# Three value blocks moved in the hand-written plan of an attention loop, and a layer norm's scale made of operations with one tensor

## What is computed

```python
xn = layernorm(x)                                  # x: 4 sequences x 1024 tokens x 1024
# s: causal attention on xn, 32 heads of 32, 8 key/value heads, rotary positions
scores = q @ k.T / sqrt(32); attn = softmax(causal(scores)); s = (attn @ v) @ wo.T
# g: a small recurrent network on the last token of each sequence (4 rows)
x_norm  = layer_norm(xn, in_gamma, in_beta)
thought = x_norm[:, -1, :] @ agg_w + agg_b
for _ in range(4):                                 # 4 steps
    t = layer_norm(thought, pn_gamma, pn_beta)     # its scale is what the change touches
    t = gelu(t @ d1_w + d1_b)                      # 1024 -> 4096
    thought = thought + (t @ d2_w + d2_b)          # 4096 -> 1024
broadcast = thought @ bc_w + bc_b
out = xn + sigmoid(xn @ gate_w + gate_b) * broadcast
g = silu(layer_norm(out, out_gamma, out_beta))
result = x + s * g
```

## Time and profile before

| | |
|---|---|
| time, median of 3 runs | 2708.13 us (2706.33 to 2709.1) |
| the profiled execution's own time | 2710.05 us |
| its span | 2708.0 us |
| PE busy | 2565.2 us, 95% |
| DVE busy | 1760.8 us, 65% |
| ACT busy | 1016.2 us, 38% |
| POOL busy | 1369.7 us, 51% |
| mean granted clock of PE | 0.978 |

### The profile page before, as it was taken

One profiled execution on the slowest core, in us unless ns is written; L12 is line 12 of the kernel. 1 busy time (PEld: TensorE's weight loads), 2 busy tenths in 40 slices (PEclk: granted clock), 3 DMA queues, 4 the chain that ended last, 5 costly groups with the idle time before them and its releaser, 6 DMA issues. The chain is left out here.

```text
span 2708.0 us, 45646 instructions
## 1 busy us (share of the span) xinstructions
PE 2565.2 (95%) x14400; PEld 1702.8 (63%) x14400; DVE 1760.8 (65%) x3577; ACT 1016.2 (38%) x1650; POOL 1369.7 (51%) x627
## 2 busy tenths in 40 slices
PE   5999999988999989999999999999859999999998
PEld 4888888863444444444444544444348888888886
DVE  6444444436676676677676676676756777777777
ACT  2111111102566656566566655665431111111111
POOL 1111111123888878988888987988711111111111
PEclk9999999997999989999999999999979999999999
DMA  6444444437456546556456555456375666655566
GB/s 239 173 179 178 173 165 163 164 119 250 154 163 189 176 134 195 160 162 188 131 178 198 166 157 182 149 167 194 114 221 117 123 128 126 119 116 116 116 116 124
DMA packets 228288, 432.05 MB, mean 160 GB/s; under 512 B 16472, under 2 KB 98520, under 8 KB 228176
## 3 DMA queue, kind: packets, MB, share of 16 engines
q1 hardware_dynamic: 154784, 378.74, 42.5%
q0 software_dynamic: 73392, 51.91, 12.6%
HBM read 316.56 MB, written 113.51 MB: 159 GB/s over the span
## 5 line engine op out<-in xcount | busy, mean ns | idle before, releaser
L883 DVE CUSTOM_DVE_ANT_0 bcast<-mxp,mask_q 128x128 f32<-128x128 f32 (+7 forms) x1054 | 753.3, 752 | 368.9 <-PE mxp L1001 192.6
L800 ACT ACTIVATE pr<-stp 128x512 f32<-128x512 f32 x1152 | 665.5, 597 | 542.8 <-PE stp L1008 343.2
L1008 PE MATMUL stp<-qs,ks 97*128 97x512 f32 x1152 | 515.1, 458 | 33.6 <-ACT pr L800 25.3
L427 PE MATMUL eo<-xt,w 128*128 128x512 f32 x1920 | 449.6, 394 | 3.6 <-DVE xt L370 3.6
L751 POOL TENSOR_TENSOR acc<-acc,pr 128x2048 f32<-128x2048 f32 x96 | 440.3, 4587 | 9.3 <-ACT pr L800 4.8
L1008 PEld LDWEIGHTS stp<-qs,ks 97*128 97x128 f32 x1152 | 216.0, 190 | 359.3 <-ACT pr L800 252.7
L427 PEld LDWEIGHTS eo<-xt,w 128*128 128x128 f32 x1920 | 359.6, 189 | 77.4 <-issue 4.0
L1371 PE MATMUL gp<-g,xa 128*128 128x512 f32 x1536 | 355.5, 391 | 17.6 <-DMA xa<-xt_scratch 17.6
L1371 PE MATMUL op<-o,ya 128*128 128x512 f32 x1536 | 355.4, 391 | 10.9 <-DVE ya L1314 10.9
L1371 PEld LDWEIGHTS gp<-g,xa 128*128 128x128 f32 x1536 | 289.8, 189 | 78.7 <-DMA xa<-xt_scratch 18.5
L1371 PEld LDWEIGHTS op<-o,ya 128*128 128x128 f32 x1536 | 289.7, 189 | 71.6 <-DVE ya L1314 11.4
(11 more groups left out here) (139 smaller groups left out, 2895.8 us busy)
## 6 DMA issues: line engine op xcount, KB each, us to landing
wch<-in_d_w SPq DMA_DIRECT2D x132, 1024.0 KB, 9.8
qs<-q_scratch SPq DMA_DIRECT2D x201, 256.0 KB, 7.3
xa<-xt_scratch POOLq DMA_DIRECT2D x66, 512.0 KB, 6.3
xt_scratch<-xt SPq DMA_DIRECT2D x16, 2048.0 KB, 14.0
q_scratch<-r SPq DMA_DIRECT2D x64, 512.0 KB, 3.2
yr<-y_scratch POOLq DMA_DIRECT2D x33, 512.0 KB, 5.8
xs<-in_x SPq DMA_DIRECT2D x33, 512.0 KB, 5.5
y_scratch<-ys SPq DMA_DIRECT2D x65, 256.0 KB, 2.0
```

Of the source, the lines that this page charges most:

```text
L427: last = nc.tensor.matmul(out, lhs[a](k), rhs[c](k), start=(k == 0 and (a, c) == (0, 0)), stop=(k == KT - 1 and (a, c) == (1, 0)))
L800: nc.scalar.activation(pr[half][:, :, at:at + P], stp[u % 2][:].rearrange("p (h t) -> p h t", h=REP), ACT.Exp, scale=SCALE).then_inc(act_d ...
L883: last = nc.vector.tensor_tensor_reduce(out=bcast[:, k % 2, hh * step:hh * step + w], in0=mxp[k % 2][:, hh * step:hh * step + w], in1=mask ...
L1008: last = nc.tensor.matmul(bank, ks[par][:, j * P:(j + 1) * P], qs[par][:, :, i * P:(i + 1) * P], start=True, stop=i != j)
```

## The change

Three value blocks stand in other slots of the plan: (1,0) goes from slot 18 to slot 22, (1,1) from 23 to 22, and (1,2) from 23 to 28. Their order doesn't change, and neither do the slots of anything else.

The layer norm's scale was three operations on 128x32 elements, each with two tensors (the second one spread out by a step of 0). It becomes four operations on 128x8 elements, one for each row r, that multiply with the one number `rs[:, r]` of each partition, and then eight on 128x4, one for each kk, that multiply with one number of each partition and add another. Only one wait of DVE for itself stands within them, where two did.

```diff
--- before.py
+++ after.py
@@ -82,17 +82,16 @@
 15: mx 6
 16: ss 1, rc 1
 17: mx 7
-18: pv 1 0
 19: mx 8, l0, lc, ge
 20: mx 9
 21: ss 0, rc 0
-22: mx 10
-23: mx 11, pv 1 1, pv 1 2
+22: mx 10, pv 1 0, pv 1 1
+23: mx 11
 24: mx 12, l1, lv
 25: mx 13
 26: mt 0
 27: mx 14
-28: mx 15, pv 1 3
+28: mx 15, pv 1 2, pv 1 3
 29: mx 16
 30: mx 17
 31: pv 1 4
@@ -858,9 +857,13 @@
 
             def layernorm_scale(k, base):
                 dve.wait_ge(ln_rs, k + 1)
-                link(nc.vector.tensor_tensor(cen[:], cen[:], rows(rs[:]), ALU.mult), base)
-                link(nc.vector.tensor_tensor(cen[:], cen[:], bc(fvec[:, 1, :], B), ALU.mult), base)
-                nc.vector.tensor_tensor(t_in[:, :, 0:B], cen[:], bc(fvec[:, 2, :], B), ALU.add).then_inc(t_done, 1)
+                for r in range(B):
+                    last = nc.vector.tensor_scalar(cen[:, :, r], cen[:, :, r], rs[:, r:r + 1], None, ALU.mult)
+                link(last, base)
+                for kk in range(KT):
+                    last = nc.vector.tensor_scalar(t_in[:, kk, 0:B], cen[:, kk, :], fvec[:, 1, kk:kk + 1],
+                                                   fvec[:, 2, kk:kk + 1], ALU.mult, ALU.add)
+                last.then_inc(t_done, 1)
 
             def reciprocals(half, k, tu):
 
@@ -1178,7 +1181,7 @@
 
 
 LINKS_TURN = 1
-LINKS_STEP = 4
+LINKS_STEP = 3
```

## The result

The changed kernel takes 2734.2 us (median of 4 runs, 2731.7 to 2736.1), the kernel before in the same comparison 2708.3 us. The ratio is 1.0097, with a 95% interval of 1.0082 to 1.0112: slower by 26 us, where 23 were forecast. The changed kernel's profiled execution took 2731.74 us, with a span of 2729.7 us, so 21.7 us more span than before.

A forecast was written before the change was run, and what follows sets the result against it. The prediction took TensorE (PE), busy for 95% of the span, to bound the kernel. It added +17 us for the moved blocks and +6 for the scale to 2708.1, giving 2731 us, range 2715 to 2743.

The forecast's parts named there:

- The block in slot 18: Value block (1,0): removing it saves nothing, as tile 9 waits for DVE's tile 7; about 1.1 us of PE left empty.
- Tile 13: In every turn, tile 13 would wait 0.54 us for its bank, because tile 11 now comes behind the pair of blocks.
- Ordinary turns: Attention turns: +1.47 us each without Gelu, -0.38 with it, the pair of blocks covering the Gelu.
- The ends of steps: Layer norm's scale there: small scalings wait for POOL's additions and free DVE later; 4 us taken.
- One to three get through in each gap: At step ends, that many of DVE's twelve scalings pass between POOL's additions; the last ones follow POOL's last addition.
- The last turns: The four last turns of a step: +1.37 us each.
- the 7.4 us: Scale's cost summed over the step ends, 0.5 + 2.7 + 2.7 + 1.5, if few operations slip through; 4 was taken.
- 17 for the plan and 6 for the scale: The forecast's two terms: moved blocks +17 us, range 13 to 21; new scale with preamble +6, bounds 0 and 16.
- the 1.4 us: At step ends the scale starts about this much later with its turn, so it was taken off DVE's delay.
- the first rival: Attention turns: the wait for DVE doesn't appear, 29.6 us are won, 2685 us; chance 0.05.
- the second: Rival at step ends: small scalings run free of POOL, 2719 us, or 2709 with the clock back; chance 0.13.
- More falls on step ends: Rival: one operation passes per gap and PE's clock stays low longer, +3 at each of four ends, 2743 us; chance 0.12.

The follow-up runs named there:

- e3: e1 with DVE's reciprocals of half 1 issued two slots later, behind tile 7: 2700.4 us, ratio 0.9965 to the kernel before.
- e5: The changed kernel with POOL's three late additions at a step end cut to four columns of each head: 2711.8 us, ratio 1.0013 to the kernel before.
- e1: The kernel before with only the three value blocks moved, the old scale kept: 2721.7 us, ratio 1.0040.
- e2: The kernel before with only the new scale, the old order of blocks kept: 2725.5 us, ratio 1.0053.
- e4: The kernel before with the Gelu one slot later, behind the exponential that score 23 waits for: 2677.1 us, ratio 0.9875.
- e9: The kernel before with the layer norm scale's three operations on POOL instead of DVE: 2691.4 us, ratio 0.9934.
- e7: The kernel before with both the later Gelu and the old scale's operations moved to POOL: 2661.6 us, ratio 0.9825.

## Why the prediction was right

**The block in slot 18.** The step on which the sign hung: its removal saves nothing, since tile 9 waits for DVE's tile 7. It held, in both kinds of turn. e3 shows the cause, the reciprocals ahead of tile 7: with them behind it the wait goes. The idle time itself is smaller than "about 1.1 us": 0.75 to 0.81 at tile 9, and in both kinds of turn 0.10 more ahead of score 19. The profile shows the block as 1.06 long, and products right behind a change of kind or a wait show 0.50 where they otherwise show 0.40, so idle time does not equal the length of what left. The difference between two starts, from which the forecast was made, does not have this fault.

**Tile 13.** Forecast 0.54 of wait, measured 0.38. The stretch from tile 9 to tile 13 was forecast as 5.93 + 0.54 = 6.47 and is 797.93 - 791.45 = 6.48 us in turn 3, and 757.94 - 751.45 = 6.49 in turn 2. Here too the sum of starts was right, and what part of it is idle was not.

**Ordinary turns.** +1.52 against +1.47 forecast, and -0.35 against -0.38. That PE needs the same time in both kinds, with the pair covering the Gelu, is seen in 39.99 and 39.92 us.

**The ends of steps.** That small scalings wait for POOL was right, and e5 shows it. "One to three get through in each gap": two start in each at the first three ends, and three, one and two in the three gaps of the last, so that the seventh is the last one held at all four. Behind score 0, tile 21 starts 1.6 us later than before at the first end (980.51 - 972.89 against 976.26 - 970.27), and 3.1 and 3.2 later at the next two, where the forecast had DVE late by 0.5 and 2.7. But the kernel before had at these two a further wait of 1.1 and 1.8 us for DVE, a few tiles on, that is gone. As whole turns the three cost 3.1 us, where 4.8 had been worked out.

Three terms were mis-sized. The last end cost 3.9 us where 1.5 stood: the forecast gave 1.2 back for the copy, which is indeed short now, 0.17 us, but the scale itself takes 10.9 us there where the old one took 6.8, 4.0 more and not 2.7, and the wait of the last products grew by 2.8. The last turns took 0.95 each, not 1.37. And of the 7.4 us worked out for the scale at the ends of steps only 4 were taken, in case more operations slipped through; they didn't.

**The two terms apart.** The prediction has 17 for the plan and 6 for the scale; alone they are 11 and 15. Most of this is one term on the other side. The forecast took the 1.4 us by which a longer turn brings the scale nearer to the end of POOL's additions off the scale, four times, 5.6 us. Measured alone, it belongs to the plan: e1's first turns of steps are shorter than those of the kernel before, with the old scale, as the changed kernel's are shorter than e2's, with the new. Put there, and with the 7.4 in place of the 4, the forecast's terms are 17 - 5.6 = 11.4 and 6 + 3.4 + 5.6 = 15.0, against 11 and 15 measured. That they agree so closely is luck, since the single terms of the table are off by up to 2.4 us, and e1's gain at two ends came in part with a drop of the clock.

The profiled executions differ by 21.7 us and the medians by 26; over these few microseconds of difference the runs can't decide, as single executions of the changed kernel lie over 4 us apart.

**The rival cases.** The wait for DVE appeared, against the first. The small scalings did not run free, against the second. "More falls on step ends" has its mark in one gap of the last end, which let one operation start; the mean clock of the first turns of steps is 0.89 in all three, where it was 0.86, 0.92 and 0.93. Its price of 12 us was not paid.

**What the change could have been.** The wait for ACT was worth 30 us, as the first rival's working says. It was to be had by moving what was late, the Gelu (e4, -34 us), and not the blocks that covered other waits. Layer norm's scale on POOL was worth 17 by itself (e9) and 13 on top of the later Gelu (e7).

## What to carry to other kernels

An engine that is busy for 38.00 of 38.00 us can still have hidden waits: before a block is moved, ask when the next instruction's buffer would be free without it, from the other engine's timeline, and work with the difference between two starts and not with idle times. To fill a wait, first try to move the late operation; work taken from elsewhere leaves a hole there. Beside an engine that keeps another one out, the number of small operations counted here and not their size, and the tiny work was best put on the engine that held the other one up. When a change is taken apart, a term can move from one half to the other, as the time at the ends of steps did here: compare the kernels turn by turn, with the clock of each turn beside it.

## What the runs showed of the hardware

- Between two additions of POOL with 0.08 us between them, two of DVE's operations start, one short and one that is held, of 8 columns as of 4. At the last end a gap of 0.15 us (1964.22 to 1964.37) let three start, and the next, 0.14 wide, only one.
- A scaling of 8 columns with one pointer takes 0.23 us, of 4 columns with two pointers 0.28 us, with starts 0.14 and 0.19 apart when nothing hinders them.
- POOL's operation on 128x32 takes 0.24 us, while its power on 128x4 takes 1.0.
- PE's granted clock also falls within single ordinary turns in which PE is busy for over 96% of the time: in the kernel before in turn 30, from 1862 us, and in e1 in turns 19, 21 and 22, of which the second row shows turn 21 (columns as in the earlier trace rows). These turns were some 1.5 us longer. Turns beside them with the same work and the same waits kept 1.00, and the cause stays open.

```profile
1862.00:1904.00 42.00, 40.42 (x264) 19.75 (x256) 27.53 (x77) 25.62 (x45) 38.06 (x13) 0.96 0.54 164
```

```profile
1504.00:1546.00 42.00, 40.69 (x261) 20.12 (x257) 27.65 (x75) 22.80 (x41) 37.03 (x13) 0.96 0.53 163
```
